# Two grouped attentions: split weights kept in DRAM, one turn more of lag, new turn tables

## The chip, the cores and the metric

One core of a Trainium2 chip runs the whole program. The time is the device time of one execution in microseconds; before and after are compared by the median of several runs.

## The reference

Four layers of cross attention and feed-forward on x, 4 batches of 256 tokens of width 256, all in float32. Two of the attentions (L1, here "a1", and L3, here "a3") are grouped: 16 query heads and 4 key/value heads of width 128. a1 rotates queries and keys by position and attends to the 1601 context rows and the 256 tokens themselves; a3 attends to the context alone. Cut to what matters (`draft_hidden` or `hidden_states` is the normalised x, the context is the same for all layers):

```python
q = rms_norm((x @ Wq).reshape(B, S, 16, 128), q_norm_w)
k = rms_norm((kv_in @ Wk).reshape(B, L, 4, 128), k_norm_w)
v = (kv_in @ Wv).reshape(B, L, 4, 128)
q, k = rope(q, pos_q), rope(k, pos_k)          # a1 alone
k, v = repeat(k, 4), repeat(v, 4)
out = softmax(q @ k.T / sqrt(128)) @ v
x = x + out.reshape(B, S, 16 * 128) @ Wo
```

## The kernel before

Both attentions are one function, `grouped_attention`; a1 has `rope` set. A group is one batch and one key/value head with its 4 query heads: 16 groups. The 1024 query columns of a group are two units of 512. The keys are 13 tiles of 128 rows (a1: 15, with 2 of tokens). A turn is one unit against one key tile, so a group has 26 turns in a3 and 30 in a1, and all engines run through the same list of turns in order.

In turn n TensorE makes the scores of turn n (three matmuls of 512 columns, since operands are split into a high and a low part), and, VALUE_LAG turns later, the product of that turn's exponentials with the values (`values`, 128x129, eight records a turn). ScalarE copies the scores into a ring of tiles (`keep`), VectorE keeps a running maximum (`highest`). After the last tile of a unit, MX transposes the maxima, VectorE reduces and negates them (`a_negmax`), NB spreads them over the partitions, and SHIFT_LAG turns after the scores GpSimd or VectorE adds them (`shift`; `by_vector` says which turns are VectorE's), EXP_LAG turns after them ScalarE takes the exponential. `outputs` on VectorE divides by the sums when a unit's values are done; in the turn in which it does so TensorE has no values, and in the next it has two turns' values.

Between these run the tasks of the neighbouring groups, named in a table of turns, GROUP_TURNS, with a `<` for a task of the group before:

- KV (keys and values of one tile for the next group), Q (queries), KN, QN (norms), KR, QR (rotation on GpSimd, a1), KX, QX (transposes of keys and queries, split into halves), OX (transposes of the outputs), Y (product with wo, added to x);
- W0, W1, W2: the split of wkv, wq and wo into `wr` halves: ScalarE copies the high half out of the staging tile `wf`, VectorE subtracts for the low one. There is one staging tile; SP waits for the low half and then loads the next weights;
- N, NZ, NX (normalised x of the next batch), PR, PX, RA, RS (positions, angles and sine tables, a1), GP and GA (gather and addition of the experts' rows for batches 1 to 3, in a1's group 0).

Items of TensorE use two PSUM banks in turn; an item waits until VectorE has taken the one before last. Each engine works in its own order, so an instruction that waits holds all behind it. A short first block (`plan_first`) prepares group 0. After the last scores the remaining values run out in a tail, with `end_turn` and `end_products` for the last group's output, and `token_statistics` for the next layer on VectorE.

The weights split as before the change, for all batches anew:

```python
def W(g, k):                       # SP
    i = splits[("W", g, k)]
    if i < len(weights):
        sp.wait_ge(w_lo, i)
        load_weights(*weights[i][1:])
```

## Time and profile before

| | us |
|---|---|
| median of 3 runs | 3647.16 (3644.31 to 3647.42) |
| profiled execution | 3644.38 |
| its span, first to last instruction | 3642.6 |
| a1, first to last score matmul | 549.5 to 1671.3 |
| a3, first to last score matmul | 2469.6 to 3488.8 |
| granted TensorE clock, mean | 0.955 |

A view of stretches gives, for each, the busy time of every engine; a view of waits says for each engine and line what it waited for last, how long in total, how often and how long at most. A matmul's end is modelled, so a stretch can hold standstill that the busy time does not show; the distance between the starts of the same instruction in successive turns does.

### The profile page before, as it was taken

The numbers are of one execution on the slowest core, as the hardware profiler recorded it, in microseconds if no ns is written. First come the engines' busy times: TensorE is split into PE (matmuls) and PEld (weight loads), VectorE is DVE, ScalarE is ACT, GpSimd is POOL, SyncE is SP. The second block draws the span as 40 slices with busy tenths as digits, with TensorE's granted clock in tenths as the row PEclk, the third lists the DMA queues.
The fourth block names the chain that finished last, engine by engine and source line by source line (L and its number), as shares of the span: only waits on it lengthen the run. The fifth ranks groups of instructions, "written<-read, shape, count | busy, mean of one in ns | idle before, by whom it ended". The sixth has DMA issues, their size and how long they took to land. (4 is left out here: it accounts for less than half of the span.)

```text
span 3642.6 us, 63987 instructions
## 1 busy us (share of the span) xinstructions
PE 3329.1 (91%) x23332; PEld 2875.7 (79%) x23332; DVE 2340.4 (64%) x4546; ACT 2299.4 (63%) x5276; POOL 1645.0 (45%) x1651
## 2 busy tenths in 40 slices
PE   6858958999999999998999999889999999999989
PEld 5658947989989988997666665578888888888888
DVE  7976746676676676665777777436655655555544
ACT  3316736777777777774567666317767677677743
POOL 0012147777777677763121020205545455454534
PEclk7879978999999999999999999899999999999999
DMA  5206521110010010002000000120010100100001
GB/s 187 91 32 224 213 70 38 33 40 24 24 49 16 24 57 16 19 13 73 37 1 37 37 1 1 75 92 27 28 48 21 54 21 21 60 21 16 16 27 38
DMA packets 57175, 175.38 MB, mean 48 GB/s; under 512 B 5860, under 2 KB 27552, under 8 KB 51872
## 3 DMA queue, kind: packets, MB, share of 16 engines
q1 hardware_dynamic: 51008, 131.90, 10.6%
q0 software_dynamic: 3696, 37.68, 2.8%
q8 instruction: 188, 3.08, 0.3%
q10 hardware_dynamic: 2160, 1.71, 0.2%
q14 instruction: 123, 1.01, 0.1%
HBM read 147.14 MB, written 24.13 MB: 47 GB/s over the span
## 5 line engine op out<-in xcount | busy, mean ns | idle before, releaser
L1159 PE MATMUL ps<-a_v_rows,a_ring 128*128 128x129 f32 (+1 forms) x7168 | 943.1, 277 | 7.8 <-ACT a_ring L1292 5.6
L1505 DVE SCALAR_TENSOR_TENSOR a_peak<-ps,a_k_rstd,a_peak 128x512 f32<-128x512 f32 (+1 forms) x768 | 575.1, 749 | 551.5 <-ACT a_ring L1277 542.3
L1396 POOL TENSOR_TENSOR a_ring<-a_ring,a_negb 128x512 f32<-128x512 f32 (+1 forms) x573 | 740.8, 1312 | 360.2 <-ACT a_negb L1286 282.1
L1159 PEld LDWEIGHTS ps<-a_v_rows,a_ring 128*128 128x128 f32 (+1 forms) x7168 | 882.9, 193 | 23.9 <-ACT a_ring L1292 9.5
L1277 ACT ACTIVATE a_ring<-ps,a_k_rstd 128x512 f32<-128x512 f32 (+1 forms) x896 | 616.3, 689 | 450.5 <-PE ps L1149 424.2
L1292 ACT ACTIVATE a_ring<-a_ring 128x512 f32<-128x512 f32 (+1 forms) x896 | 563.8, 632 | 12.1 <-DVE a_ring L1522 6.4
L1147 PE MATMUL ps<-a_qt,a_kt 128*128 128x512 f32 (+1 forms) x896 | 427.1, 477 | 5.0 <-PEq L73 5.0
L1045 PEld LDWEIGHTS ps<-a_wr,a_ct 128*128 128x128 f32 (+1 forms) x2496 | 351.7, 189 | 73.8 <-DVE a_k_rows L1474 22.3
L1045 PE MATMUL ps<-a_wr,a_ct 128*128 128x256 f32 (+1 forms) x2496 | 375.0, 288 | 31.3 <-DMA a_ct<-ctx_lo 16.0
L1149 PE MATMUL ps<-a_qt,a_kt 128*128 128x512 f32 (+1 forms) x896 | 358.0, 400 | 0.0
L1148 PE MATMUL ps<-a_qt,a_kt 128*128 128x512 f32 (+1 forms) x896 | 356.7, 398 | 0.0
L3361 ACT ACTIVATE a_probs<-ps 128x1024 f32<-128x1024 f32 x224 | 229.7, 1026 | 135.7 <-PE ps L3215 134.9
L3553 DVE TENSOR_REDUCE a_parts<-ps 128x1 f32<-128x448 f32 x384 | 222.3, 619 | 57.2 <-PE ps L3177 51.9
L1522 DVE TENSOR_TENSOR a_ring<-a_ring,ps 128x512 f32<-128x512 f32 x323 | 218.4, 678 | 2.9 <-ACT a_negb L1286 2.8
L1149 PEld LDWEIGHTS ps<-a_qt,a_kt 128*128 128x128 f32 (+1 forms) x896 | 167.6, 187 | 43.4
L1147 PEld LDWEIGHTS ps<-a_qt,a_kt 128*128 128x128 f32 (+1 forms) x896 | 170.9, 191 | 7.3 <-issue 5.6
L1148 PEld LDWEIGHTS ps<-a_qt,a_kt 128*128 128x128 f32 (+1 forms) x896 | 170.9, 191 | 1.6
L3215 PE MATMUL ps<-a_qt,a_kt 128*128 128x512 f32 x448 | 164.2, 448 | 2.5 <-ACT a_qt L3348 2.3
L1432 DVE TENSOR_TENSOR a_wr<-a_wf,a_wr 128x1024 fp32r<-128x1024 f32 (+1 forms) x88 | 131.6, 1496 | 52.7 <-ACT a_wr L1220 52.6
L3177 PE MATMUL ps<-a_kt,a_qt 128*128 128x448 f32 (+1 forms) x512 | 154.8, 369 | 4.6 <-ACT a_kt L3329 1.2
L1474 DVE TENSOR_TENSOR a_k_rows<-ps,a_kw 128x128 f32<-128x128 f32 (+1 forms) x448 | 126.3, 283 | 45.7 <-ACT a_v_rows L1240 45.4
L1331 POOL TENSOR_SCALAR a_k_sq<-a_k_sq 128x4 f32<-128x4 f32 (+2 forms) x128 | 26.2, 205 | 285.8 <-ACT a_v_rows L1240 281.1
(468 smaller groups left out, 6201.0 us busy)
## 6 DMA issues: line engine op xcount, KB each, us to landing
a_wf<-in_a_wo SPq DMA_DIRECT2D x32, 512.0 KB, 3.6
a_wf<-in_a_wq SPq DMA_DIRECT2D x28, 512.0 KB, 3.6
a_ct<-ctx_hi SPq DMA_DIRECT2D x8, 1090.0 KB, 5.6
a_ct<-ctx_lo SPq DMA_DIRECT2D x8, 1090.0 KB, 8.3
f_we<-in_f_experts SPq DMA_DIRECT2D x8, 1088.0 KB, 8.4
a_wf<-in_a_wkv SPq DMA_DIRECT2D x28, 256.0 KB, 2.6
ctx_hi<-a_ct SPq DMA_DIRECT2D x4, 1602.0 KB, 5.4
ctx_lo<-a_ct SPq DMA_DIRECT2D x4, 1602.0 KB, 9.3
```

The lines of the kernel that those rows point to most:

```text
L1045: ins = pe.matmul(out[0:r, 0:2 * HD], src, wr[0][v][:, c * 2 * HD:(c + 1) * 2 * HD], start=(n == 0), stop=(n == 3 * DC - 1))
L1147: pe.matmul(out, kt[0][:, at:at + r], qt[0][:, cols], start=True, stop=False)
L1148: pe.matmul(out, kt[0][:, at:at + r], qt[1][:, cols], start=False, stop=False)
L1149: pe.matmul(out, kt[1][:, at:at + r], qt[0][:, cols], start=False, stop=True).then_inc(st_ready, 1)
L1159: ins = pe.matmul(m.ps[:, 6 + i // 2, (i % 2) * 256:(i % 2) * 256 + VW], slot(n)[0:r, i * P:(i + 1) * P], v_rows[u // NG % 2][0:r, t, :], ...
L1277: act.activation(slot(n)[0:r, :], m.ps[0:r, SCORE_BANKS[n % 3], :], ACT.Copy, scale=k_rstd[0:r, g % 2, t:t + 1]).then_inc(kept, 1)
L1292: act.activation(slot(n)[0:r, :], slot(n)[0:r, :], ACT.Exp).then_inc(exp_done, 1)
L1396: pool.tensor_tensor(slot(n)[0:r, :], slot(n)[0:r, :], negb[0:r, u % 2, :], ALU.add)\
L1505: dve.scalar_tensor_tensor(out=peak[0:r, :], in0=m.ps[0:r, SCORE_BANKS[n % 3], :], scalar=k_rstd[0:r, u // NG % 2, t:t + 1], in1=(slot(n - ...
L1522: dve.tensor_tensor(slot(n)[0:r, :], slot(n)[0:r, :], m.ps[0:r, MAX_BANK, :], ALU.add)\
L3361: act.activation(flat2(probs[n % 3][:, :, :]), flat2(m.ps[:, first:first + 2, :]), ACT.Exp)\
L3553: dve.tensor_reduce(to, slot(("R", h, j))[:, 0:n], AX.X, ALU.max, negate=True).then_inc(neg_done, 1)
```

## The change

- SP writes both halves of each split weight to DRAM (`kept_w`) while batch 0 is worked on. From then on the tasks W are fetches: SP reads both halves back into `wr` once the last user is done, ScalarE and VectorE do nothing, and TensorE waits for the landing. ScalarE's next split into the same `wr` waits for the stores, and SP's next load stands behind them.
- SHIFT_LAG, EXP_LAG, VALUE_LAG and the ring are one turn longer; both tables are new; the gathered rows use `o_rows` in place of a tile `y_in`.
- In the last unit VectorE has two of three shifts (before, every second). At the end, the first half's output is turned at END_TURN, and its low half, its products and the statistics come at END_LOW, after the last shift.
- The first maximum of a unit waits until the maxima of the unit before are transposed.

```diff
-        "QX1< MX1", "NB1 KR6<", "Q0 KR7<", "RA3", "Q1 RA4 PR0 GP4", "KX3< RA5 GP5", "OX0 QN0 RA6 GA4 GP6",
-        "KV0 W1 RA7 PX0 GA5 GP7", "KV1 QN1 RA8 GA6 GP8", "KV2 RA9 GA7 GP9", "KV3 RS0 RA0 GA8 GP10", "KV4 GA9 GP11",
-        "KV5 KN0 QR0 RA1 GA10 GP12", "KV6 QR1 GA11 GP13", "KV7 QR2 RA2 GA12 GP14",
-        "KV8 MX0 QR3 GA13 GP15", "NB0 KN1 KR0 GA14", "QX0 KR1 GA15", "KV9 KR2", "KX0 KV10", "KV11 KR3 N0", "OX1",
-        "Y0 KN2", "KX1 NZ0", "Y1 KR4", "KV12 KR5 W2", "KV13", "KV14", "KX2", "W0 KN3 NX0",
+        "QX1<", "MX1 KR6<", "NB1 KR7<", "Q0 RA3", "RA4 PR0 GP4", "RA5 GP5", "Q1 RA6 GA4 GP6",
+        "KX3< RA7 PX0 GA5 GP7", "KV0 QN0 W1 RA8 GA6 GP8", "OX0 KV1 RA9 GA7 GP9", "KV2 QN1 RS0 RA0 GA8 GP10", "KV3 GA9 GP11",
+        "KV4 KN0 QR0 RA1 GA10 GP12", "KV5 QR1 GA11 GP13", "KV6 QR2 RA2 GA12 GP14", "KV7 QR3 GA13 GP15",
+        "MX0 KN1 KR0 GA14", "NB0 KV8 KR1 GA15", "QX0 KR2", "KV9 KR3", "KX0 KV10", "KV11 N0", "KV12",
+        "OX1 KX1 KN2", "Y0 NZ0", "KV13 KR4", "Y1 KR5", "KV14", "W2", "KX2 W0 KN3 NX0",
...
-        "QX1< MX1", "NB1", "KX3<", "Q0", "", "Q1", "OX0", "KV0 QN0 W1", "KV1", "KV2 QN1", "KV3", "KV4 N0", "KV5 KN0",
-        "KV6 MX0", "NB0 QX0 NZ0", "KV7", "KV8 KN1", "KX0", "KV9", "OX1 KV10", "Y0", "KX1 KV11", "Y1 KN2", "KV12 W2",
-        "KX2", "W0 KN3 NX0",
+        "QX1<", "MX1", "NB1 KX2< KN3<", "Q0", "KX3<", "", "Q1", "QN0", "OX0 KV0 W1", "KV1 QN1", "KV2", "KV3 N0", "KV4 KN0",
+        "KV5 QX0", "MX0 KV6 NZ0", "NB0", "KV7", "KX0 KV8", "KN1", "KV9", "KV10", "OX1 KX1", "Y0",
+        "KV11 KN2", "Y1 W2", "KV12 W0 NX0",
...
     TURNS = GROUPS * T
-    SHIFT_LAG, EXP_LAG, VALUE_LAG = KT + 2, KT + 4, KT + 5
+    SHIFT_LAG, EXP_LAG, VALUE_LAG = KT + 3, KT + 5, KT + 6
     RING = VALUE_LAG + 2
     SCORE_BANKS, MAX_BANK = (0, 1, 4), 5
-    END_AT = TURNS + VALUE_LAG - KT + 1
+    END_TURN, END_LOW = TURNS + VALUE_LAG - KT + 3, TURNS + SHIFT_LAG
     KB = [(t0, min(t0 + 4, KT)) for t0 in range(0, KT, 4)]
...
         if rope:
-            y_in = st.sb("y_in", [P, QT, D])
             cs = st.sb("cs", [P, 2, KT, half])
...
+        kept_w = [[nc.dram_tensor(f"{name}_w{k}{i}", (KVH, P, n), F32, kind="Internal").ap() for i in range(2)]
+                  for k, n in enumerate(WIDTHS)]
+        w_out = [st.sem(f"w_out{k}") for k in range(3)]
         norm_in, zeroed = st.sem("norm_in"), st.sem("zeroed")
...
             u, t = divmod(n, KT)
-            return t % 4 == 3 if not rope and u < UNITS - 1 else t % 2 == 1
+            if u == UNITS - 1:
+                return t % 3 > 0
+            return t % 2 == 1 if rope else t % 4 == 3
...
             acted = {task: i + 1 for i, task in enumerate(t for t in items if t[0] not in ("PX", "Y", "MX"))}
-            weights = [t for t in flat if t[0] == "W"]
+            weights = [t for t in flat if t[0] == "W" and (not attend or t[1] < (KVH if t[2] == 2 else KVH - 2))]
+            fetches = [t for t in flat if t[0] == "W" and t not in weights]
             splits = {task: i + 1 for i, task in enumerate(weights)}
...
-                return (z, y_in)[j % 4 // 2][:, j % 2, :]
+                if j % 4 < 2:
+                    return z[:, j % 2, :]
+                return flat2(o_rows[:, 2 * (j % 2):2 * (j % 2) + 2, :])
...
-            def split_at(g, k):
...
-                return splits.get(("W", g - 1, k), 0)
+            def head_of(g, k):
...
+                return (g + 2) % KVH if k < 2 else g % KVH
...
+            def stores(g, k):
...
+                return sum(1 for _w, h, i in weights if i == k and h < g) + (1 if attend and k < 2 else 0)
...
+            def wait_weights(pe, g, k):
...
+                task = ("W", g - 1, k)
+                if task in splits:
+                    pe.wait_ge(w_lo, splits[task])
+                elif task in fetches:
+                    mine = [t for t in fetches if t[2] == k]
+                    pe.wait_ge(pre[k], 16 * sum(1 for t in weights if t[2] == k) + 32 * (mine.index(task) + 1))
...
-                        sp.dma_start(staged(g, k), (w["wkv"], w["wq"], w["wo"])[k][(g + 2) % KVH if k < 2 else g % KVH])\
-                            .then_inc(pre[k], 16)
+                        sp.dma_start(staged(g, k), (w["wkv"], w["wq"], w["wo"])[k][head_of(g, k)]).then_inc(pre[k], 16)
...
+                    def store_weights(g, k):
...
+                        for i in range(2):
+                            sp.dma_start(kept_w[k][i][head_of(g, k)], wr[k][i][:, :].bitcast(F32)).then_inc(w_out[k], 16)
...
+                    def fetch_weights(g, k):
...
+                        last = {0: ("KV", g, KT - 1), 1: ("Q", g, QT - 1), 2: ("Y", g, QT - 1)}[k]
+                        sp.wait_ge(item_ready, number[last] + 1)
+                        sp.wait_ge(w_out[k], 32 * stores(g, k))
+                        for i in range(2):
+                            sp.dma_start(wr[k][i][:, :].bitcast(F32), kept_w[k][i][head_of(g, k)]).then_inc(pre[k], 16)
...
                             sp.wait_ge(w_lo, splits[("W", KVH - 2, k)])
+                            store_weights(KVH - 2, k)
                             load_weights(KVH - 1, k)
...
                             sp.wait_ge(pre[k], 32)
+                            sp.wait_ge(w_out[k], 32)
                         return
...
+                        if ("W", g, k) in fetches:
+                            fetch_weights(g, k)
+                            return
                         i = splits[("W", g, k)]
+                        sp.wait_ge(w_lo, i)
+                        store_weights(g, k)
                         if i < len(weights):
-                            sp.wait_ge(w_lo, i)
                             load_weights(*weights[i][1:])
...
                     load_weights(*weights[0][1:])
+                    for k in (0, 1):
+                        store_weights(KVH - 1, k)
                     if rope:
...
                             pe.wait_ge(peaked, peaks(TURNS - 1))
-                            pe.wait_ge(w_lo, splits[("W", GROUPS - 1, 2)])
+                            wait_weights(pe, GROUPS, 2)
                         pe.wait_ge(end_lo, k + 1)
...
                                 values(v)
-                        if attend and n == END_AT:
+                        if attend and n == END_TURN:
                             end_turn(0)
-                        if attend and n == END_AT + 2:
+                        if attend and n == END_LOW:
                             end_products(0)
...
-                        if loaded(g, k):
-                            act.wait_ge(pre[k], 16 * loaded(g, k))
+                        if ("W", g, k) in fetches:
+                            return
+                        act.wait_ge(pre[k], 16 * loaded(g, k))
+                        if stores(g, k):
+                            act.wait_ge(w_out[k], 32 * stores(g, k))
                         if k == 2 and ("Y", g, 1) in number:
...
                     def W(g, k):
+                        if ("W", g, k) in fetches:
+                            return
                         dve.wait_ge(w_hi, splits[("W", g, k)])
...
                             dve.wait_ge(peaked, peaks(n - 1))
+                        elif u:
+                            dve.wait_ge(item_ready, number[("MX", u // NG, 1 - u % NG)] + 1)
                         dve.scalar_tensor_tensor(out=peak[0:r, :], in0=m.ps[0:r, SCORE_BANKS[n % 3], :],
```

The other lines of the diff let KV, Q, Y and the end wait through `wait_weights`, and put END_TURN and END_LOW in the place of END_AT on the other engines.

## Rows read from the trace of the kernel before

**Rows 1.** The page: TensorE's busy time, and the second halves of the weight splits
```profile
PE 3329.1 (91%) x23332; PEld 2875.7 (79%) x23332; DVE 2340.4 (64%) x4546; ACT 2299.4 (63%) x5276; POOL 1645.0 (45%) x1651
...
L1432 DVE TENSOR_TENSOR a_wr<-a_wf,a_wr 128x1024 fp32r<-128x1024 f32 (+1 forms) x88 | 131.6, 1496 | 52.7 <-ACT a_wr L1220 52.6
```

**Rows 2.** Stretches, group by group: length, engines' busy us, TensorE clock, DMA share, GB/s
```profile
549.47:615.41 65.94, 55.20 (x296) 46.86 (x297) 41.00 (x69) 41.18 (x111) 53.92 (x55) 0.84 0.15 45
615.41:1617.81 1002.40, 979.90 (x7061) 892.68 (x7059) 678.86 (x1155) 754.61 (x1892) 736.79 (x746) 1.00 0.09 29
903.44:973.43 69.99, 69.51 (x506) 63.75 (x505) 45.56 (x79) 52.85 (x136) 51.79 (x54) 1.00 0.06 20
...
758.78:833.48 74.70, 70.38 (x506) 63.51 (x505) 52.50 (x87) 57.37 (x140) 52.88 (x54) 1.00 0.05 19
...
2515.32:3441.56 926.24, 879.76 (x6245) 804.36 (x6244) 542.83 (x918) 658.33 (x1684) 485.36 (x466) 0.98 0.10 31
2780.16:2844.70 64.54, 61.79 (x448) 56.47 (x447) 38.27 (x65) 46.96 (x121) 34.53 (x33) 1.00 0.07 21
...
2644.10:2714.17 70.07, 63.43 (x448) 58.24 (x447) 38.52 (x65) 47.37 (x121) 34.56 (x33) 0.95 0.10 36
```

**Rows 3.** TensorE's timeline in a3, group 5: first score matmuls of five turns
```profile
2835.80 0.48 PE L1147 MATMUL ps<-a_qt,a_kt 128*128 128x512 f32 x1
...
2838.80 0.48 PE L1147 MATMUL ps<-a_qt,a_kt 128*128 128x512 f32 x1
...
2841.09 0.47 PE L1147 MATMUL ps<-a_qt,a_kt 128*128 128x512 f32 x1
...
2843.12 0.47 PE L1147 MATMUL ps<-a_qt,a_kt 128*65 128x512 f32 x1
...
2844.70 0.48 PE L1147 MATMUL ps<-a_qt,a_kt 128*128 128x512 f32 x1
```

**Rows 4.** Waits of TensorE in a3 (2463 to 3513): total us, times, longest
```profile
PE ps L1126 <- DVE a_negmax L1513: 20.8, 12, 2.0
PE ps L1115 <- DVE a_zt L1445: 16.0, 3, 6.1
PE ps L1045 <- DVE a_k_rows L1474: 8.7, 15, 1.0
```

**Rows 5.** Waits of ScalarE in a3 (2515 to 3442), for the staged wkv
```profile
ACT a_wr L1220 <- DMA a_wf<-in_a_wkv: 37.0, 14, 5.8
```

**Rows 6.** Timeline in a3, group 0: the W2 split, the next load, the W0 split
```profile
2511.52 1.05 ACT L1220 ACTIVATE a_wr<-a_wf 128x1024 fp32r<-128x1024 f32 x1
...
2514.00 0.33 SPq L960 DMA_DIRECT2D a_wf<-in_a_wkv  x1
...
2516.60 0.63 ACT L1220 ACTIVATE a_wr<-a_wf 128x512 fp32r<-128x512 f32 x1 [1.20 <-DMA a_wf<-in_a_wkv]
```

**Rows 7.** Waits of TensorE in a1 (549 to 1677)
```profile
PE ps L1092 <- DVE a_o_rows L1531: 8.4, 15, 1.5
PE ps L1075 <- POOLq L1360: 7.0, 4, 3.1
```

**Rows 8.** DMA issues in a3 (2463 to 3495): KB each, median us to landing
```profile
a_wf<-in_a_wkv SPq DMA_DIRECT2D x14, 256.0 KB, 2.6
...
a_ct<-ctx_hi SPq DMA_DIRECT2D x3, 512.0 KB, 4.0
a_ct<-ctx_lo SPq DMA_DIRECT2D x3, 512.0 KB, 4.8
```

**Rows 9.** Timeline of a1's tail: GpSimd's and VectorE's last additions, end of the values
```profile
1676.65 9.89 POOL L1396 TENSOR_TENSOR a_ring<-a_ring,a_negb 128x512 f32<-128x512 f32 x8 [17.88 <-ACT a_negb L1286]
...
1687.10 3.08 DVE L1522 TENSOR_TENSOR a_ring<-a_ring,ps 128x512 f32<-128x512 f32 x5
...
1697.74 0.18 DVE L1530 RECIPROCAL a_rsum<-ps 128x4 f32<-128x4 f32 x1 [7.56 <-PE ps L1159]
```

More of the change, by code:

```diff
@@ L1035, in KV @@
                         if t == 0:
-                            if split_at(g, 0):
-                                pe.wait_ge(w_lo, split_at(g, 0))
+                            wait_weights(pe, g, 0)
                         if t in (0, 4) and g % KVH == KVH - 1:
@@ L1052, in Q @@
                         out = begin(("Q", g, q))
-                        if split_at(g, 1):
-                            pe.wait_ge(w_lo, split_at(g, 1))
+                        wait_weights(pe, g, 1)
                         if g in norms and q == 0:
@@ L1096, in Y @@
                         out = begin(("Y", g, q))
-                        if split_at(g, 2):
-                            pe.wait_ge(w_lo, split_at(g, 2))
+                        wait_weights(pe, g, 2)
                         pe.wait_ge(item_free, number[("OX", g, 1)] + 1)
@@ L1313, in _ @@
                                 does[task](g, i)
-                        if attend and n == END_AT:
+                        if attend and n == END_TURN:
                             end_high(0)
@@ L1600, in _ @@
                                 does[task](g, i)
-                        if attend and n == END_AT:
+                        if attend and n == END_LOW:
                             end_low(0)
```

## The prediction

> **What bounds the kernel now.** I read the page first: TensorE is busy 91% of the span, far ahead of the rest [rows 1]. Then the busy time of each engine, group by group, in the two stages that the change touches [rows 2]: a1 (groups 1 to 14: 1002.4 us, TensorE busy 979.9 at full clock) and a3 (926.2 us, busy 879.8, clock 0.98). VectorE, ScalarE and GpSimd are at 50 to 75% there. So work taken from them is worth nothing in itself; the time is TensorE's own work plus what it stands still. Busy time is modelled, so I measure the standstill by turns. In a quiet part of an a3 group the starts of the first score matmul lie 3.00, 2.29, 2.03 and 1.58 us apart [rows 3]: turns with Y1, KV12, KX2 and nothing but scores and values. Hence a bare turn is 1.59, a KV adds 0.70, a Y (and, as long, a Q) 1.42, each transpose or spread item 0.44. An a3 group is 26 x 1.59 + 13 x 0.70 + 4 x 1.42 + 11 x 0.44 + 0.1 (KX3 turns 65 columns) = 61.1 us of work; an a1 group 30 x 1.59 + 15 x 0.70 + 5.7 + 11.8 x 0.44 = 69.1. Measured are 64.5 for a usual a3 group and 70.0 for a usual a1 group, 70.1 and 74.7 where the batch changes [rows 2]. Over groups 1 to 14: a3 926.2 - 14 x 61.1 = 70.8 us of standstill, a1 1002.4 - 14 x 69.1 = 35.0.
>
> **Who makes it.** In a3 TensorE's list of waits is led by NB waiting for the negated maxima (20.8 us, 12 times), MX waiting for the low half that NX's bank holds (16.0 in three waits, 6.1 the longest) and KV waiting for the drain of its bank (8.7, 15 times) [rows 4]. The first two have one cause: ScalarE waits 14 times, 37.0 us in all, for wkv to land in the single staging tile [rows 5]. The W2 split begins at 2511.52, VectorE's half ends, SP issues the wkv load at 2514.00, ScalarE gets it at 2516.60 [rows 6]. Behind ScalarE stand W0's low half and then the reduction of MX1 on VectorE, which NB1, one turn later on TensorE, needs. Where the wait is 5.8 us (the load lies behind a context load), the group takes 70.1 us, 5.5 above the usual one [rows 2, 5]. The third is OX1 and KV10 in a turn in which VectorE also forms the outputs. In a1 the wkv load has four turns and there is no such wait; the rows are OX0 on the outputs of the turn before (8.4) and KX0 on GpSimd's rotation (7.0) [rows 7].
>
> **The change, part by part.**
> *Splits.* Of 14 + 14 + 16 splits a stage, 12 + 12 + 12 go: 72 pairs of a ScalarE copy and a VectorE subtraction of 1.5 us mean [rows 1]. Neither engine is the bound; their own worth is 0. What counts is the in-order wait for the staging tile. From batch 1 on, SP reads both halves from DRAM into the weight tiles, and only TensorE waits, 8 turns (18 us) later for wkv and over 20 turns later for wo. Two transfers of 512 KB issued together land after 4.0 and 4.8 us [rows 8], so each fetch is covered. At the change of batch in a3 they follow 2.1 MB of context and, in batch 0, also 1.5 MB of wo: at the pair's 1 MB in 5.4 us some 16 us together, against 18. I charge 2 us once.
> *One more turn of lag, items spread.* NB1 now stands a turn after MX1, OX0 and OX1 a turn after the double values turn, QX0 and KX0 a turn further from the rotation. So NB's, OX's and most of KX's waits lose their cause. The lag adds no matmul: the first group has one values turn fewer and the tail one more.
> *a3, groups 1 to 14*: 70.8, less 3 NX items that are work (1.3), less what I leave standing (about 0.3 us a group, 4, and the 2 above) = 63.5 back, before the next item. From nothing to 69.
> *a1, groups 1 to 14*: 35.0, less 1.6 of items for the new batch, less 10 for the three groups in which the sine tables and the angles of the next batch fill ScalarE and VectorE (74.7 against 70.0, [rows 2], and that work stays) = 23.4 back. From 12 (the two causes that rows name, half of each) to 33.
> *The new wait: batch 0.* Here the splits stay, and SP stores both halves before it issues the next load. W2 and W0 now stand in neighbouring turns, in both tables, in groups 0 and 1: four events. From W2's start SP's first store is issued 2.5 us later [rows 6]; the stores land 5.4 us after that (the second of a pair is issued 0.6 later and takes 4.8), and 256 KB behind them take 0.7 more (a pair's second half costs 1.4 for 512 KB) [rows 8]: 8.6 us after W2's start. ScalarE is at W0 after 2.7 us (a turn, its exp, copy and KX2 or KV12), so it waits about 5.9 us. Queued behind it are the exp and copy of the next turns, and behind those values, scores and NB. The trace has this price: the 5.8 us wait made a group of 70.1 instead of 61.1 + 0.4 of NX, that is some 8 us at TensorE, slower clock (0.95) included [rows 2, 5]. With the NB a turn further off I take 7, from 3.5 (the load is not held by the stores) to 9. Four events: -28 (-14 to -36).
> The Trainium skill (DMA: Bandwidth & Descriptors, Anatomy of one DMA) gives a transfer 2.0 us plus its bytes at 436 GB/s: 2.6 for 256 KB, which the trace has (2.6), and as an estimate 5.0 us for stores and load together where I have 6.1; by it each event would be 1 us cheaper and the sum 4 us lower.
> *First groups.* a1's takes 65.9 us for some 46 of work, much of it for GpSimd, which issues the gathers and rotates queries [rows 2]. GP6 and GP7 now go before QN0, which helps; 1.5 MB of stores at the start of the block share the DMA engines with the gathers, which hurts. I take 2 back (-4 to +8); in a3, without gathers or rotation, 2 for the items spread. The stores in the short first blocks land before W1 and W0 want theirs: 0.
> *Last group and tail.* Group 15 has the usual waits: 1 + 2 back. In the tail VectorE's statistics stood before its last five additions (they ran from 1687.10), while GpSimd did eight in 9.9 us; values ended at 1697.74 [rows 9]. Now the statistics come after the last addition and GpSimd has 5 of 15 (and 5 of 13). After the last scores (1672.2) TensorE has 20 turns of values (17.8) and 2.8 of items; it took 25.5. The wait for the outputs of the half-group before stays: 2.5 back in each stage, between 0 and 4.
> *o_rows in place of y_in, the wait of the first maximum on MX*: MX's transposes come right after the scores, the maximum waits for ScalarE's copy anyway: 0, at worst 0.2 x 30 in each stage.
>
> **The sum.** 63.5 + 23.4 - 28 + 4 + 3 + 5 = 70.9. The profiled execution took 3644.4 (1.8 outside its span); 3644.4 - 70.9 = 3573.5. The median of the runs shown lies 2.8 above it: 3576.3, say 3576.
>
> **Rivals.**
> 1. *The stores don't hold the load.* It lands 1.0 + 2.6 us after the first store's issue; the wait is 3.5, the price 3.5 instead of 7: 3562. For it: reads and writes may overlap. Against it: two loads of a pair clearly share the rate [rows 8].
> 2. *The waits come back elsewhere.* VectorE has 0.75 + 0.68 of maximum and addition in a 1.59 turn, and OX1 with KX1 (both tables) gives it two low halves in one, before a Y. Were half of the 87 us to return as waits for k_rows, a_ot or a_negmax, 3619. For it: KV's waits on k_rows [rows 4]; against it: VectorE is 59% busy in a3 and loses 1.9 us of splits a group.
> 3. *No change.* The four events cost 25 us each instead of 7, which needs the load to land 18 us later than worked out. Nothing in the rows does that to 1.25 MB.
> 4. *Slower: fetches come late.* The 24 groups with fetches read 61 MB instead of half of it. If W0's fetch lands after KV0 is due, TensorE itself stands. Place: KV0. It has 18 us, and decides from an overrun of 71/24 = 3 us in every group; at 5 us the time is 3576 + 24 x 5 = 3696. Against it: DMA engines are busy 6 to 19% of these groups [rows 2].
>
> **How the numbers follow.** Likeliest 0.62, with its own range 3555 to 3605 (the bounds of the events, +8 to -14, and of the first groups and tails, +-10, hardly all at once). Rival 1 0.14 (3545 to 3570), rival 2 0.15 (3600 to 3635), rival 3 0.03, rival 4 0.06. The range 3548 to 3622 leaves out a little of rival 1, half of rival 2, and the last two: under 2 in 10. What a measurement can tell from no change is 0.2%, 7 us. Faster 0.91, same 0.03, slower 0.06.
>
> **What would show it.** Right: ScalarE's waits for wkv only in groups 0 and 1 of a3 (and now of a1), 5 to 6 us each; groups 2 and later of a3 at 61 to 62 us, of a1 at 69; no NB wait on the maxima outside those four places; the three groups of a1 with tables still above 72; DMA traffic some 50 MB higher and no wait of KV, Q or Y on it; in the tail one unbroken run of VectorE additions. Wrong: a3 groups at 63 and more with waits on k_rows or the low halves (rival 2), KV0 waiting on a DMA (rival 4), or the four events at 3 us (rival 1) or at 10 and more.

## The result and the profile after

The changed kernel takes 3652.2 us (median of 20 runs, 3650.2 to 3658.4) against 3644.2 for the kernel before (20 runs): ratio 1.002, 95% interval 1.0014 to 1.0027. It is 8 us slower: little, but the interval does not reach 1. Its profiled span is 3651.7 us. The prediction was 3576 us, faster, and neither the time nor the sign came out.

The page of the changed kernel:

```profile
PE 3330.9 (91%) x23332; PEld 2863.2 (78%) x23332; DVE 2248.3 (62%) x4479; ACT 2251.3 (62%) x5204; POOL 1628.3 (45%) x1646
```

VectorE loses 92 us and ScalarE 48 against [rows 1]: the splits are gone. TensorE has as much to do as before.

The stretches answer to [rows 2]. In order: a1's first group; a1 groups 1 to 14; group 5 (a usual one); group 7 (before a change of batch); a3 groups 1 to 14; group 4; group 1 (columns as there):

```profile
543.42:607.32 63.90, 51.52 (x288) 43.13 (x289) 38.98 (x67) 40.00 (x109) 52.08 (x54) 0.91 0.24 83
607.32:1660.03 1052.71, 995.64 (x7061) 896.52 (x7059) 641.58 (x1121) 732.03 (x1857) 734.97 (x746) 0.99 0.14 48
921.26:993.03 71.77, 69.93 (x506) 63.55 (x505) 42.01 (x76) 51.20 (x132) 51.74 (x54) 1.00 0.11 38
1067.37:1146.98 79.61, 71.87 (x506) 63.46 (x505) 49.83 (x84) 54.60 (x136) 51.88 (x54) 1.00 0.10 34
...
2555.86:3446.61 890.75, 871.68 (x6246) 795.48 (x6244) 488.50 (x886) 635.15 (x1651) 478.10 (x467) 0.99 0.16 56
2758.75:2821.24 62.49, 61.76 (x448) 56.39 (x447) 33.91 (x62) 44.91 (x118) 34.56 (x35) 1.00 0.15 53
2555.86:2627.48 71.62, 65.34 (x448) 59.37 (x447) 39.27 (x66) 47.38 (x123) 36.88 (x34) 0.93 0.16 56
```

The two stages went opposite ways. a3 is 35.5 us shorter over its 14 groups; a usual group is 62.5, which was forecast at 61 to 62. a1, which was to be shorter, is 50.3 us longer: its usual group has gone from 70.0 to 71.8 and group 7, before a change of batch, from 74.1 to 79.6. Some 15 of the 50 are the two batch-0 events, which were forecast apart. So the question is a1.

TensorE's waits in a1 (543 to 1716), us in total, times, longest:

```profile
PE ps L1163 <- DVE a_negmax L1557: 27.6, 31, 4.3
PE ps L1196 <- ACT a_ring L1332: 10.9, 5, 3.7
PE ps L1084 <- DVE a_k_rows L1516: 10.8, 12, 2.6
```

Before, [rows 7] were led by the outputs and by KX0. OX's wait for the outputs is gone from the list, as forecast. NB (now L1163) waited 4.0 us in 13 times before; now it waits at 31 of 32 places. A second difference stands one engine away, in ScalarE's waits in a1 (607 to 1660), where the exponentials (L1332) wait for GpSimd's additions (L1436):

```profile
ACT a_ring L1332 <- POOL a_ring L1436: 54.1, 51, 2.6
...
ACT a_wr L1260 <- DMA a_wf<-in_a_wkv: 10.6, 2, 5.3
```

In the kernel before, the same wait came to 3.6 us in 6 times. The wkv row is one of the batch-0 events that were forecast; in a3 (2555 to 3446) it is

```profile
ACT a_wr L1260 <- DMA a_wf<-in_a_wkv: 12.1, 2, 7.4
```

where [rows 5] had 37.0 us in 14 waits. Where NB's wait comes from is seen in the timeline of a1's group 5, VectorE's and TensorE's own lines (start, duration, what it did):

```profile
959.00 0.60 PE L1152 MATMUL ps<-ident,a_peak 128*128 128x128 f32 x4
...
959.92 0.75 DVE L1549 SCALAR_TENSOR_TENSOR a_peak<-ps,a_k_rstd,a_ring 128x512 f32<-128x512 f32 x1 [1.45 <-ACT a_ring L1317]
...
960.59 0.68 DVE L1566 TENSOR_TENSOR a_ring<-a_ring,ps 128x512 f32<-128x512 f32 x1
...
961.18 0.68 DVE L1557 TENSOR_REDUCE a_negmax<-ps 128x4 fp32r<-128x512 f32 x1
...
961.92 0.66 PE L1163 MATMUL ps<-ident_r,a_negmax 128*128 128x128 f32 x4 [0.73 <-DVE a_negmax L1557]
```

MX's transposes (L1152) are done at 959.60 and VectorE is idle, but its program has the running maximum (L1549) first, which waits for ScalarE's copy of this turn's scores, then an addition (L1566), and only then the reduction (L1557). Before, MX stood in a unit's first turn, the only one that has no running maximum. The change moved it to the second.

### The profile page after: what moved, and what is told of

Read it like the earlier page. It is cut to its first block and busy times, and to the rows that moved or that the text cites. A ratio compares the mean times of both kernels' runs of the same rounds, so it can differ in the third digit from the quotient of the medians.

```text
span 3651.7 us, 64134 instructions
## 1 busy us (share of the span) xinstructions
PE 3330.9 (91%) x23332; PEld 2863.2 (78%) x23332; DVE 2248.3 (62%) x4479; ACT 2251.3 (62%) x5204; POOL 1628.3 (45%) x1646
## 5 line engine op out<-in xcount | busy, mean ns | idle before, releaser
L1549 DVE SCALAR_TENSOR_TENSOR a_peak<-ps,a_k_rstd,a_peak 128x512 f32<-128x512 f32 (+1 forms) x768 | 575.9, 750 | 628.0 <-ACT a_ring L1317 619.9
L1436 POOL TENSOR_TENSOR a_ring<-a_ring,a_negb 128x512 f32<-128x512 f32 (+1 forms) x568 | 723.2, 1294 | 307.8 <-ACT a_negb L1326 296.7
L1332 ACT ACTIVATE a_ring<-a_ring 128x512 f32<-128x512 f32 (+1 forms) x896 | 562.8, 631 | 64.8 <-POOL a_ring L1436 57.4
L1084 PE MATMUL ps<-a_wr,a_ct 128*128 128x256 f32 (+1 forms) x2496 | 377.8, 289 | 32.2 <-DMA a_ct<-ctx_lo 16.7
L1084 PEld LDWEIGHTS ps<-a_wr,a_ct 128*128 128x128 f32 (+1 forms) x2496 | 345.7, 188 | 73.0 <-issue 17.1
L1566 DVE TENSOR_TENSOR a_ring<-a_ring,ps 128x512 f32<-128x512 f32 x328 | 220.8, 677 | 2.8 <-ACT a_negb L1326 2.8
L1516 DVE TENSOR_TENSOR a_k_rows<-ps,a_kw 128x128 f32<-128x128 f32 (+1 forms) x448 | 126.2, 283 | 65.3 <-ACT a_v_rows L1280 64.6
L1276 ACT ACTIVATE a_square<-ps 128x128 f32<-128x128 f32 (+1 forms) x448 | 124.5, 278 | 52.5 <-PE ps L1084 46.8
```

The costliest lines, as they stand in the source:

```text
L1084: ins = pe.matmul(out[0:r, 0:2 * HD], src, wr[0][v][:, c * 2 * HD:(c + 1) * 2 * HD], start=(n == 0), stop=(n == 3 * DC - 1))
L1332: act.activation(slot(n)[0:r, :], slot(n)[0:r, :], ACT.Exp).then_inc(exp_done, 1)
L1436: pool.tensor_tensor(slot(n)[0:r, :], slot(n)[0:r, :], negb[0:r, u % 2, :], ALU.add)\
L1549: dve.scalar_tensor_tensor(out=peak[0:r, :], in0=m.ps[0:r, SCORE_BANKS[n % 3], :], scalar=k_rstd[0:r, u // NG % 2, t:t + 1], in1=(slot(n - ...
L1566: dve.tensor_tensor(slot(n)[0:r, :], slot(n)[0:r, :], m.ps[0:r, MAX_BANK, :], ALU.add)\
```

## The experiments

Each kernel is the changed one unless said otherwise. "Group" lengths are from one first score matmul of a group to the next, as in [rows 2]. All were timed beside the kernel before, and the ratios are to it. Its own median was 3644.0 us beside experiments 1 to 4, 3643.2 beside 5 to 8, 3646.3 beside 9, 3640.9 beside 10 and e15_w2_early, and 3646.8 beside e16_y0_later. So a difference of a few us between kernels of different groups is read with the ratios and with the lengths of stages in the traces. In the diffs `...` stands for lines left out.

**1. VectorE's reduction ahead of the running maximum (e1_mx_first).**

```diff
+ for task, g, i in turn:
+     if task == "MX": MX(g, i)
  if attend and n < TURNS and n % KT: highest(n)
...
```

> The changed kernel, but in the turn of an MX task VectorE reduces the transposed maxima before it takes the turn's running maximum and its addition, not behind them. Theory A (the new tables put MX into a turn in which VectorE has a maximum and an addition to do first, so that NB on TensorE waits): NB's waits on a_negmax go, usual groups of a1 fall from 71.8 to about 69.8, of a3 from 62.4 to about 61.2; some 45 us less than the changed kernel, near 3605. Rival B (the waits are set by ScalarE's and GpSimd's lateness, the order on VectorE only shows it): the wait moves to the exponentials or to a_ot and less than 10 us come back, 3642 or more.

3642.0 us, ratio 0.9994 (0.9984 to 1.0005): 10 us back, and only 0.3 in a usual a1 group (71.5). That is far from theory A's 3605. The time is rival B's, but not its mechanism: the wait did not go to another engine's lateness. TensorE's waits in a1 groups 1 to 14 show what took its place; NB no longer waits for the reduction but for VectorE's addition (in this kernel L1566):

```profile
PE ps L1163 <- DVE a_ring L1566: 14.7, 28, 0.5
```

NB overwrites the bank that VectorE's additions of the unit before read, so it waits for the last of these, too. That addition was also moved a turn by the longer SHIFT_LAG, and so it stands in the same turn as MX, behind the running maximum. Experiment 5 follows this up.

**2. SP issues the next load ahead of the stores (e2_load_first).**

```diff
  sp.wait_ge(w_lo, i)
- store_weights(g, k)
  if i < len(weights): load_weights(*weights[i][1:])
+ store_weights(g, k)
```

> The changed kernel, but in batch 0 SP issues the next weights' load before the two stores of the weights just split. Theory A (the four places where W0 follows W2 cost 7 to 8 us each because wkv lands behind 1 MB of stores): ScalarE's waits for wkv fall from 5 to 7 us to 2 to 3, groups 1 and 2 of a1 from 79.8 and 81.7 to about 75 to 77, the same two in a3 from 71.6 and 68.8 to about 65; 18 to 22 us less than the changed kernel, about 3632. Rival B (the wait is that of the load alone, adjacent turns are enough): under 6 us back.

3636.7 us, ratio 0.9984 (0.9975 to 0.9994), 15.5 us below the changed kernel, a little less than theory A's 18 to 22. The four groups take 2.8 to 4.1 us less each (a1 77.0 and 77.8, a3 67.5 and 65.2), which is about half of what an event costs. The stores do hold the load. SP's and ScalarE's timelines of the changed kernel, where the first event of a3 stands, show by how much: the W2 split, the two stores with the load behind them, the W0 split.

```profile
2553.56 1.05 ACT L1260 ACTIVATE a_wr<-a_wf 128x1024 fp32r<-128x1024 f32 x1
...
2563.57 0.63 ACT L1260 ACTIVATE a_wr<-a_wf 128x512 fp32r<-128x512 f32 x1 [7.45 <-DMA a_wf<-in_a_wkv]
```

```profile
2556.92 0.80 SPq L985 DMA_DIRECT2D a_w<-a_wr  x2
2557.75 0.79 SPq L980 DMA_DIRECT2D a_wf<-in_a_wkv  x1
```

The load is there 10.0 us after W2's start (8.6 were predicted) and 6.65 after the first store's issue; in a1's first event these are 7.9 and 5.0 us (605.26 and 608.19 to 613.17). By the fit of the Trainium skill (DMA: Bandwidth & Descriptors, Anatomy of one DMA), which the page gives for transfers that GpSimd issues, the prediction estimated 5.0 us for the latter: a1's event agrees with it, a3's does not.

**3. The kernel before with only the weights kept in DRAM (e3_keep_only).** Old tables, lags, ring, tail and VectorE's old share of the additions.

```diff
- SHIFT_LAG, EXP_LAG, VALUE_LAG = KT + 3, KT + 5, KT + 6   # and the tables
+ SHIFT_LAG, EXP_LAG, VALUE_LAG = KT + 2, KT + 4, KT + 5
```

> The kernel before with only the split weights kept in DRAM and fetched (tables, lags, ring length, by_vector and the end as before). Theory A (keeping the weights is worth what the staging waits cost in a3, and a1's loss is made by the new tables): a3 40 to 50 us shorter than before, a1 within 5 us of before (in its old table W0 has four turns), 3644 - 45 = about 3600. Rival B (stores and fetches slow a1 by contention): a1 longer by 20 us or more, total 3640 or more.

**4. The changed kernel without it (e4_tables_only).** All weights are loaded and split in every batch; nothing is stored.

```diff
- weights = [t for t in flat if t[0] == "W" and (not attend or t[1] < (KVH if t[2] == 2 else KVH - 2))]
+ weights = [t for t in flat if t[0] == "W"]
...
```

> The changed kernel without the weights kept in DRAM: every group's weights are loaded and split again, tables, lags and the end as changed. Theory A: a1's loss of some 35 us outside the four places stays and a wait of 2 to 3 us of ScalarE for wkv comes in each of 14 groups (W2 and W0 in neighbouring turns), a1 55 to 75 us longer than before; a3 about as before or longer by up to 20: 3700 to 3740. Rival B (the stores and fetches make a1's loss, the tables are good): a1 no longer than before, total 3650 or less.

3600.7 us (ratio 0.9889, 0.9866 to 0.9911) and 3714.6 us (1.0205, 1.0181 to 1.0230), theory A by the time in both. This splits the change in two: keeping the weights is worth 44 us alone, and the tables with their lag and the new end cost 70 alone. The halves don't add: they would make 27 us of loss, and the change has 8. With the weights kept, most of the places are gone where the new tables wait for a split. Groups 1 to 14 of a1 and of a3 with the weights kept and the old tables:

```profile
609.32:1608.69 999.37, 978.83 (x7060) 893.46 (x7059) 635.63 (x1120) 731.62 (x1857) 736.71 (x746) 1.00 0.14 49
...
2506.04:3394.99 888.95, 870.05 (x6245) 797.04 (x6244) 488.99 (x884) 634.58 (x1649) 472.99 (x466) 0.99 0.16 56
```

a3 has its whole gain (926.2 to 889.0) without any new table, a1 3 us. With the new tables and every weight split anew, a3's 14 groups take 910.8 us, 15.4 less than before, where theory A had none or a loss; a1's take 1094.9, 92.5 more, where it had 55 to 75. ScalarE waits for wkv 33.2 us in 14 waits in a3, where [rows 5] had 37.0, and 40.8 in 14 in a1, where the old table had 1.3 in 2. So in a1, where W2 and W0 had four turns between them, putting them into neighbouring turns makes a wait wherever a split is left.

**5. Reduction, then addition, then running maximum (e6_shift_first).** As experiment 1, and in MX's turn VectorE's addition comes ahead as well.

```diff
+ early = any(task == "MX" for task, g, i in turn)
+ if early and attend and 0 <= s < TURNS and by_turn[s]: shift(s)
  if attend and n < TURNS and n % KT: highest(n)
...
```

> The changed kernel with VectorE's order in MX's turn altered once more: reduction of the maxima, then VectorE's shift, then the running maximum (the run before moved only the reduction and gave 3642.0 us). Theory A: what is left of NB's wait is the last shift that VectorE does for the half-group before. NB overwrites the bank which that shift reads, and with one more turn of lag the shift stands in MX's turn, behind the running maximum. That is 14.7 us in a1 over 28 NBs, and some 0.6 in one turn of each a3 group, 8 us: 3617 to 3623 us, a usual a1 group at 70.5, an a3 group at 61.5. Theory B: the reduction and the shift are now limited by MX's transposes and the drain, and another wait stands right behind: above 3632 us.

3614.7 us, ratio 0.9920 (0.9903 to 0.9936), 27 below experiment 1, theory A and 2 us better. a3's groups are at 61.3, a1's at 70.9, and NB's wait in a1's groups 1 to 14 is down to 0.2 us. Against the changed kernel both edits took 19.5 us from a3's groups 1 to 14 and only 14.9 from a1's. The turns of a1's group 5 show where the rest went: turns 2 and 17, which hold NB, fell from 3.03 and 3.74 to 2.15 and 2.86 us, but turns 20 and 21 rose from 2.76 and 1.59 to 3.38 and 1.81. With NB's wait gone another one came up there; experiment 10 finds it. VectorE's timeline in the turn of MX, group 6 of a1:

```profile
990.73 0.69 DVE L1557 TENSOR_REDUCE a_negmax<-ps 128x4 fp32r<-128x512 f32 x1 [0.52 <-PE ps L1152]
991.34 0.68 DVE L1566 TENSOR_TENSOR a_ring<-a_ring,ps 128x512 f32<-128x512 f32 x1
991.94 0.74 DVE L1549 SCALAR_TENSOR_TENSOR a_peak<-ps,a_k_rstd,a_ring 128x512 f32<-128x512 f32 x1
```

**6. KX1 out of OX1's turn (e7_kx1_apart).** On experiment 5.

```diff
- "KV12", "OX1 KX1 KN2",      # a1
+ "KV12 KX1", "OX1 KN2",
- "KV10", "OX1 KX1",          # a3
+ "KV10 KX1", "OX1",
```

> The run e6_shift_first, and KX1 one turn ahead of OX1 instead of in the same turn, in both tables. Theory A: Y0 waits 0.64 us in each a1 group because VectorE makes the low halves of OX1 and KX1 back to back; it comes back 16 times, 10 us below e6_shift_first (3610 us); nothing in a3, where the two turns together show no loss. Theory B: the same VectorE work is now late for the KV item and its drain in the turn before: within 3 us of e6_shift_first.

3646.4 us, ratio 1.0006 (0.9996 to 1.0016): 32 us above experiment 5, which neither theory had. Its waits say a part of why. In a1 (616 to 1640) Y0 (L1141) waits twice as long for OX1's halves (5.4 us in 14 waits before), as I read it since the work in OX1's turn that covered it is gone; in a3 (2550 to 3480) KX1 itself (L1113) now waits for its keys:

```profile
PE ps L1141 <- DVE a_ot L1487: 10.7, 13, 0.8
...
PE ps L1113 <- DVE a_k_rows L1516: 5.6, 15, 2.3
```

In a usual a1 group, 0.7 us longer (71.6), the turn with Y0 takes 4.08 us instead of 3.63. The turn that KX1 came into rose by 0.75 and the one that it left fell by 0.45, where a transpose item is 0.44 of work.

**7. KR3 a turn later (e8_kr3_later).** On experiment 6.

```diff
- "KV9 KR3", "KX0 KV10",
+ "KV9", "KX0 KV10 KR3",
```

> The run e7_kx1_apart, and in a1 the second half of GpSimd's second rotation of keys (KR3) one turn later, as far from the first half as in the table before. Theory A: GpSimd's four neighbouring turns of rotation hold its shifts, so that ScalarE's exponentials and then the values wait, most in the four groups before a change of batch (turn 20 takes 4.9 us instead of 3.0): 6 to 9 us below e7_kx1_apart. Theory B: these groups are held by VectorE's angle work and by KX0's own wait for the first rotation: at most 3 us below.

3649.2 us, ratio 1.0012 (1.0002 to 1.0022): no gain, theory B; a usual a1 group went from 71.6 to 71.9. As I read it, the move gives GpSimd no time and only reorders what it is late with.

**8. The load ahead of the stores on top (e9_all_mended).** The same edit as in experiment 2, on experiment 7.

> The run e8_kr3_later, and SP issues the next load of a staging tile ahead of the stores of the weights just split (which alone was worth 15.5 us in the changed kernel). Theory A: the effects add up, 12 to 18 us below e8_kr3_later, 3582 to 3595 us, below the 3600.7 of the kernel before with weights kept. Theory B: with shorter turns the load has less time and the stores still hold it: less than 8 us, above 3600 us.

3635.7 us, ratio 0.9973 (0.9963 to 0.9982): 13.6 us below e8_kr3_later, the step of theory A, but from a start some 45 us above the 3601 to 3604 that was expected, so that its total is 40 us above theory A's.

**9. Four more.** e13_shift_load is experiment 5 with the load first. e12_kx0_later is that, with KX0 a turn later in a1. e10_keep_load_first is experiment 3 with the load first. e11_old_a1_mended has a3 as in e13_shift_load, and a1 with the code and the table of the kernel before.

```diff
- "KX0 KV10", "KV11 N0", "KV12",          # e12_kx0_later
+ "KV10", "KX0 KV11 N0", "KV12",
```

> The changed kernel with the order of e6_shift_first (3614.7 us) and the load ahead of the stores. Theory A: both effects add (the second was 15.5 us alone): 3598 to 3602 us. Theory B: the shorter turns leave the same wait, less than 8 us: above 3607 us.

> The changed kernel with the order of e6_shift_first, the load ahead of the stores, and in a1 KX0 one turn later (turn 21 instead of 20). Theory A: KX0 waits there for GpSimd's rotation of the first keys (its two turns take 5.9 us where the work is 5.0, and 7.6 in the groups before a change of batch), and a turn later it waits for nothing: 15 to 20 us below e13_shift_load, 3578 to 3587 us. Theory B: what is late is GpSimd's shifts, not the rotation, or KX0's drain now meets KX1's: within 5 us of e13_shift_load.

> The kernel before with the split weights kept in DRAM (old tables and lags; that alone was 3600.7 us, with 69.4 and 69.6 us in groups 1 and 2 of a3 against 62.4 in the later ones), and SP issues the next load ahead of the stores. Theory A: the stores hold the load here too, and the two groups give back 4 us each: 3590 to 3595 us. Theory B: in the old tables W2 and W0 stand two turns apart, so the load lands in time either way and the 14 us are the old wait for wkv: 3598 us or more.

> a3 with the changed kernel's code, the order of e6_shift_first and the load ahead of the stores; a1 with the whole code and table of the kernel before (weights loaded and split in every batch). Theory A: the stages add: a1 1121 us as before, a3 961.6 - 7 = 955, the rest as it was: 3568 to 3578 us, the fastest version. Theory B: part of a1's length in the changed kernel does not come from its table and lag and comes back here, or a3 is longer: above 3588 us.

e13_shift_load: 3607.2 us, ratio 0.9901 (0.9884 to 0.9917), theory B. It is 7.4 us below experiment 5, and the gain is in a3 (871.2 to 864.7 us over groups 1 to 14); in a1 groups 1 and 2 gain 3.6, and the first group and those before a change of batch lose about as much, so the effects don't simply add there. e10_keep_load_first: 3593.2 (0.9861, 0.9842 to 0.9880), theory A. e11_old_a1_mended: 3577.7 (0.9821, 0.9804 to 0.9838), theory A: the stages add. With experiment 3, in which kept weights didn't lengthen a1 under its old table, this puts a1's loss on its table and lag. e12_kx0_later: 3619.6 (0.9930, 0.9914 to 0.9947), 12 us slower than its base, a miss for both theories. The 5.9 us that its expectation gives for KX0's two turns are those of group 6; in a usual group they take 5.2 for 5.0 of work, and KX0 waits for the rotation only 6 times in the stage (6.6 us), so there was little to win. KX0's own wait went, and the items behind it wait instead; in its list for a1 (616 to 1640) KV (L1084) waits for KX0's low half (a_kt), which before it did not:

```profile
PE ps L1084 <- DVE a_k_rows L1516: 13.1, 17, 1.6
PE ps L1084 <- DVE a_kt L1487: 13.0, 13, 1.0
```

**10. GpSimd's rotation starts earlier (e14_qr0_first).** On e13_shift_load. After three tries at the end of GpSimd's chain or behind it, this one is at its beginning. GpSimd's timeline of e13_shift_load, group 5, its first instruction of the chain and the last one that KX0 needs (turn 20 starts at 960.14):

```profile
941.76 0.20 POOL L1371 TENSOR_SCALAR a_k_sq<-a_k_sq 128x4 f32<-128x4 f32 x1 [4.04 <-ACT a_v_rows L1280]
942.04 1.04 POOL L1372 TENSOR_TENSOR a_k_rstd<-a_k_sq,nhalf 128x4 f32<-128x4 f32 x1
943.05 1.29 POOL L1391 TENSOR_TENSOR a_by_sin<-a_q_rows,a_cs 128x512 f32<-128x512 f32 x1
...
959.70 0.74 POOL L1399 TENSOR_TENSOR a_k_rows<-a_by_cos,a_by_sin 128x256 f32<-128x256 f32 x1
```

It stands 4.04 us until ScalarE has copied KV3, and from then on works almost without a pause for over 20 us. In this group KX0 does not wait for it. What waits is ScalarE's exponential, for the addition that GpSimd does behind the rotation:

```profile
960.92 0.60 PE L1113 MATMUL ps<-ident,a_k_rows 128*128 128x128 f32 x4
...
961.90 0.63 ACT L1332 ACTIVATE a_ring<-a_ring 128x512 f32<-128x512 f32 x1 [1.18 <-POOL a_ring L1436]
```
 The new table has KV3 in turn 11 instead of 10, and KN0, which needs it, still in turn 12 ahead of QR0, which does not.

```diff
- "KV4 KN0 QR0 RA1 GA10 GP12",
+ "KV4 QR0 KN0 RA1 GA10 GP12",
```

> The run e13_shift_load (3607.2 us), with GpSimd's first rotation of queries (QR0) ahead of the statistics of the first keys (KN0) in the same turn of a1. Theory A: in the groups before a change of batch GpSimd stands 10.2 us until ScalarE has copied KV3, which in the new table comes a turn later and so behind the sine tables; the eight neighbouring turns of rotation start 3 us late, and KX0 pays it. With QR0 ahead the chain starts when the sines are there, 2.7 us earlier: groups 3, 7 and 11 of a1 give back 2 to 3 us each (79.5 to about 77), 6 to 8 us in all. Theory B: GpSimd's chain is too long for its turns wherever it starts, or the time comes from VectorE's angle work: under 2 us in all.

3583.3 us, ratio 0.9851 (0.9834 to 0.9867), 24 below its base by the medians and 18 by the ratios; the traces put 24.7 into a1's groups 1 to 14. Theory A had 6 to 8. The groups 3, 7 and 11 gave 9.6, and each usual group about 1 us more, which theory A had not: its effect holds for every group. The same last rotation, of the same group:

```profile
941.91 0.73 POOL L1399 TENSOR_TENSOR a_k_rows<-a_by_cos,a_by_sin 128x256 f32<-128x256 f32 x1
```

That is 3.0 us before turn 20 (944.89), where it had begun 0.4 before it; turns 20 and 21 went from 3.41 and 1.80 us to 2.74 and 1.48. The exponentials' wait for GpSimd in a1 (607 to 1650), and a1 groups 1 to 14, a usual one and group 7:

```profile
ACT a_ring L1332 <- POOL a_ring L1436: 11.4, 12, 1.2
```

```profile
604.02:1614.98 1010.96, 982.27 (x7060) 892.32 (x7059) 643.20 (x1121) 728.59 (x1857) 734.72 (x746) 1.00 0.14 50
899.61:969.49 69.88, 69.49 (x507) 63.63 (x505) 42.05 (x76) 50.77 (x132) 51.66 (x54) 1.00 0.12 39
1041.27:1117.43 76.16, 71.29 (x506) 63.50 (x505) 49.85 (x84) 54.65 (x136) 51.87 (x54) 1.00 0.10 36
```

The exponentials had waited 65.0 us, 50 times, in e13_shift_load; that stage was 1035.7 us there, and is 24.7 shorter.

**11. W2 a turn earlier in a1 (e15_w2_early), and KV13 between OX1 and Y0 (e16_y0_later).** Each on the one before.

```diff
- "KV14", "W2", "KX2 W0 KN3 NX0",              # e15_w2_early
+ "KV14 W2", "", "KX2 W0 KN3 NX0",
- "Y0 NZ0", "KV13 KR4", "Y1 KR5",              # e16_y0_later
+ "KV13 NZ0", "Y0 KR4", "Y1 KR5",
```

> The run e14_qr0_first, with a1's W2 one turn earlier (turn 27, two turns ahead of W0 instead of one). Theory A: what is left of the cost of batch 0 in a1 (groups 1 and 2 at 74.1 and 79.0 us against 70.9 and 73.4 in later batches, with the load ahead of the stores) comes from W2 and W0 standing in neighbouring turns: half or more of these 8.8 us back, 4 to 8 us in all. Theory B: it is the stores themselves, which ScalarE waits for before it overwrites the split weights: nothing (within 1.5 us).

> The run e15_w2_early (3579.2 us), with KV13 and Y0 exchanged in a1, so that a KV item instead of a bare turn stands between OX1 with KX1 and Y0. Theory A: Y0 waits 0.4 us in each group (14 times, 5.4 us) for OX1's low half, which VectorE forms beside KX1's, and its turn is 3.6 us where the work is 3.0; one item between gives the low half a turn: 6 to 10 us below e15_w2_early, 3569 to 3573 us. Theory B: as with KX1 moved apart, the wait moves to the next item, now Y1 and Y0 back to back and KV13 behind KX1's low half: within 3 us, or longer.

e15_w2_early: 3579.2 us, ratio 0.9827 (0.9811 to 0.9843). The medians differ by 4 us, within the spread of either, but groups 1 and 2 of a1 went from 73.3 and 75.1 to 71.0 and 72.6: 4.8 us in the traces, the low end of theory A. e16_y0_later: 3576.2 us, ratio 0.9807 (0.9790 to 0.9823), 3 below by the medians, and a1's groups 1 to 14 are 1.4 us shorter; theory B. The turn with Y0 lost its wait (3.62 to 3.00 us), and the turn with KV13 took it (2.30 to 2.86); a usual group is 69.8 instead of 69.9. The row of the wait is now KV13's, in a1 (543 to 1700):

```profile
PE ps L1084 <- DVE a_ot L1487: 5.3, 17, 0.4
```

and a1 and a3, groups 1 to 14:

```profile
607.95:1611.82 1003.87, 981.88 (x7061) 892.30 (x7059) 638.87 (x1120) 729.17 (x1856) 735.61 (x747) 1.00 0.14 50
...
2505.57:3370.20 864.63, 860.23 (x6245) 791.44 (x6244) 488.38 (x886) 632.17 (x1651) 478.03 (x467) 1.00 0.16 58
```

## Why the prediction was wrong

**The step that failed** is "One more turn of lag, items spread: ... So NB's, OX's and most of KX's waits lose their cause", and with it a1's 23.4 us back. a1 lost 50.3, of which 15.4 are its two events; the other 34.9 stand against the 23.4 and make 58 of the 80 us by which the two spans (3642.6 and 3651.7) missed the sum. OX's part held. NB's did not: in a1 its wait rose from 4.0 to 27.6 us. I looked at the distance between items in TensorE's list and not at what each engine's own in-order queue has in the turn an item is moved to. The parts won back, each by the run that did it, in the order in which the edits were stacked (with another order the shares would differ: GpSimd's delay costs a usual group of a1 0.1 us in turns 20 and 21 as long as NB's wait is there):

| part | where it was undone | us |
|---|---|---|
| NB behind the running maximum and the moved addition | a1 and a3, both edits of experiment 5 | 37.5 (3652.2 to 3614.7) |
| GpSimd's chain starts at KV3's copy, now a turn later | a1, experiment 10 | 24 (18 by ratios) |
| the stores ahead of the load | a3, e13_shift_load | 7.4 |
| W2 next to W0 | a1, e15_w2_early | 4 to 5 |

Together they make 76 with the last 3 of e16_y0_later: the table, with these orders mended, takes 3576.2 us.

**NB.** I wrote that "NB1 now stands a turn after MX1". It always did; the lag moved both, and moved them from a unit's first turn, where VectorE has no maximum to take, to its second. Of [rows 4] the 20.8 us of NB's wait in a3 went where the splits went: experiment 3 leaves 11.0, of which 8.4 are in the two groups that still split and 2.0 in groups 3 to 14. The changed kernel has 12.6, of which 8.7 are in its groups 3 to 14: that is what the new order put back.

**KX.** "QX0 and KX0 a turn further from the rotation" is true of KX0 and KR1 in the table. But GpSimd's rotation doesn't start where the table has it: it starts when KV3 is copied, and that moved with it. In group 5 of a1 the chain starts 18.3 us before KX0's turn in the kernel before and 18.4 in e13_shift_load. Rival 2, "the waits come back elsewhere" (3619), was the nearest in kind, and a_negmax is in its list. But it gave VectorE's load as the cause and not its order, and looked at OX1 and KX1, where experiment 6 shows that taking the pair apart costs time. It also took 1.9 us of VectorE's work a group as saved by the splits; in a3 it is 3.9 (542.8 to 488.5 over 14 groups). GpSimd, with eight turns of rotation in a row, was not weighed at all: one rotation with an addition takes it 5.4 us (943.05 to the start of the next at 948.46), for two turns of 2.3. Its 45% of the span said nothing about these turns.

**a3** was to give 63.5 over groups 1 to 14, with two events of 7 and the first and last groups beside. It gave 35.5 with the events in it. Taking those as 9.2 and 5.9 (71.6 and 68.8 us against 62.4 and 62.9 in later groups of their kind) leaves 50.6, 13 too little. NB's order more than accounts for it: the two edits of experiment 5 took 19.5 us out of these groups. In e13_shift_load the groups are at 61.3, the floor of 61.1 that [rows 3] gave.

**The four events** were priced about rightly: 7 each predicted, 8.0 and 7.4 in a1, 9.2 and 5.9 in a3 over the later groups of their kind, 30.5 in all for 28. Rival 1 (the stores don't hold the load) is refuted by experiment 2, rival 4 (late fetches) by the lists of waits: no item of TensorE waits for a fetch, at a DMA share of 0.16. The measured time is in no rival's range. That it is slower at all (chance 0.06) was forecast only by way of late fetches, which did not happen.

**First and last groups, tails.** The first groups gave 2.0 and 2.5 back (4 predicted), the last ones took 2.4 and 2.2 more (3 back predicted) with NB and the additions as above. From the last score matmul to the last outputs a1's tail went from 26.5 to 25.8 us and a3's from 24.7 to 23.7: 1.7 back, where 5 was predicted; no run asks why. What is left of the difference between the two spans is some 4 us less outside these terms. In the changed kernel's trace a1 begins 6.1 us earlier, but over all the traces its start varies between 540.4 and 549.8 us, so that says nothing of the change.

**What stays open.** In a1 the groups before a change of batch stand at 76.1 us in the best version, at 73.9 with the kernel before's code (e11_old_a1_mended) and at 73.2 with the old table and kept weights (experiment 3). Turns 7, 9 and 12 stand out (4.1, 4.1 and 3.7 us where a usual group has 2.7, 2.8 and 2.3), and no run moved these. That moves of KX1 and KX0 by one turn cost 32 and 12 us is measured, with the wait that came up; that this wait is all of it was not shown. Part of experiment 10's gain may be TensorE's clock (below), which was not measured apart.

**The best versions** are e16_y0_later (3576.2) and e11_old_a1_mended (3577.7), which differ by less than can be told. Keeping the weights alone makes 44 of the 68 us, and 51 with the load ahead of the stores.

## What to carry to other kernels

When a table moves an item by a turn, write down for every engine the whole list of that turn in program order, not only the distance to the consumer: a position can be good because something is absent there. For an engine that rotates or adds in a chain, find the event that starts the chain and its slack at the end; an edit at the start was worth 24 us where three among the items at the end gained nothing or cost time. And time a change that has two parts in halves: one half here was worth 44 us and the other cost 70 without it.

## What the runs showed of the hardware

A stand of several microseconds costs TensorE more than itself. The event of a3's group 1 in the changed kernel, in stretches of 5 us (length, TensorE's busy us, granted clock, DMA share, GB/s):

```profile
2555.00:2560.00 5.00, 4.27 (x32) 1.00 0.47 181
2560.00:2565.00 5.00, 0.23 (x1) 0.76 0.28 84
2565.00:2570.00 5.00, 4.22 (x16) 0.50 0.62 210
2570.00:2575.00 5.00, 5.00 (x25) 0.72 0.01 2
2575.00:2580.00 5.00, 5.00 (x35) 1.00 0.00 0
```

TensorE does next to nothing from 2560 to 2565, and then runs at the lower of its two levels (0.50, 1.2 GHz) through the next stretch and part of the one after: eight value matmuls that take 1.05 us elsewhere took 2.09 there. Over the group that makes 65.3 us of TensorE work against 61.8 in group 4 for the same 448 matmuls. In e13_shift_load, where ScalarE's wait is short, group 1 takes 64.6 us with a clock of 1.00 and 61.7 of work. So a wait of some 5 us on TensorE cost about 3.5 more, an estimate from these groups. Over a1's 14 groups TensorE's busy time rose from 979.9 to 995.6 us with the change and fell from 994.8 to 982.3 in experiment 10. Not all of that is the clock: a usual group's fell from 70.1 to 69.5 with 1.00 in both, since a matmul's modelled end holds some standstill.

The fetches cost nothing that a wait shows: 96 of 512 KB landed in 4.1 us and 48 of 256 KB in 3.6 (median), beside context loads and stores, with a DMA share that went from 0.10 to 0.16 in a3. The DMA engines moved 227.8 MB instead of 175.4, the 50 MB more that were forecast.
